# Moving 32x32-turned probability blocks from buffer to buffer in 16 transfers instead of through DRAM

## The reference, cut to what matters

```python
scores = jnp.einsum('bqhd,bkhd->bhqk', q[..., :DN], k) * scale
scores = jnp.where(causal[None, None], scores, NEG_INF)
probs = jax.nn.softmax(scores, axis=-1)
attn = jnp.einsum('bhqk,bkhd->bqhd', probs, v).reshape(B, S, H * DV)
return jnp.einsum('bse,ed->bsd', attn, wo)
```

## Time and profile before

| | us |
|---|---|
| median of 3 runs | 1063.7 (1060.49 to 1066.61) |
| the profiled execution's own time | 1062.6 |
| its span, from the first to the last instruction | 1060.7 |
| TensorE busy | 1047.7 |
| VectorE, GpSimd, ScalarE busy | 808.9, 754.8, 543.0 |

### The profile page before, as it was taken

One profiled execution on the slowest core, in us unless ns is written; L12 is line 12 of the kernel. 1 busy time (PEld: TensorE's weight loads), 2 busy tenths in 40 slices (PEclk: granted clock), 3 DMA queues, 4 the chain that ended last, 5 costly groups with the idle time before them and its releaser, 6 DMA issues. The chain is left out here.

```text
span 1060.7 us, 19733 instructions
## 1 busy us (share of the span) xinstructions
PE 1047.7 (99%) x6025; PEld 918.1 (87%) x6025; DVE 808.9 (76%) x1959; ACT 543.0 (51%) x1573; POOL 754.8 (71%) x1030
## 2 busy tenths in 40 slices
PE   9999999999999999999999999999999999999998
PEld 8888878898898898878988898889888888888987
DVE  7598974467688687877888787878788778778775
ACT  4454321033764555556555555555556555555663
POOL 4777568897957875977597668848774876587920
PEclk9999999999999999999999999999999999999999
DMA  5111242110232333334333423342434333333412
GB/s 168 51 49 52 97 143 70 60 46 21 76 99 82 115 115 99 98 102 132 80 97 118 133 82 96 104 135 75 126 86 123 87 113 111 105 92 109 119 55 79
DMA packets 108120, 100.67 MB, mean 95 GB/s; under 512 B 72688, under 2 KB 88240, under 8 KB 107888
## 3 DMA queue, kind: packets, MB, share of 16 engines
q1 hardware_dynamic: 107728, 98.89, 31.5%
q10 hardware_dynamic: 288, 0.52, 0.1%
HBM read 74.26 MB, written 25.10 MB: 94 GB/s over the span
## 5 line engine op out<-in xcount | busy, mean ns | idle before, releaser
L2063 ACT ACTIVATE prob<-prob,top 128x128 f32<-128x128 f32 (+1 forms) x256 | 114.2, 448 | 85.2 <-DVE top L2096 84.6
L1724 POOL TENSOR_TENSOR form_lo<-wqk_stage,form_hi 128x256 fp32r<-128x256 f32 x192 | 143.5, 748 | 16.0
L2069 ACT ACTIVATE prob<-prob,inv 128x128 f32<-128x128 f32 (+1 forms) x256 | 102.8, 450 | 51.1 <-DVE inv L2102 51.1
L1778 POOL TENSOR_SCALAR vf_hi<-wvo_stage 128x512 fp32r<-128x512 f32 (+1 forms) x48 | 26.6, 554 | 117.4 <-PE banks L200 85.2
L198 PE MATMUL banks<-tT_hi,form_hi 128*128 128x512 f32 x256 | 103.7, 405 | 0.8 <-DVE qT_lo L1851 0.5
L199 PE MATMUL banks<-tT_lo,form_hi 128*128 128x512 f32 x256 | 100.0, 391 | 0.0
L200 PE MATMUL banks<-tT_hi,form_lo 128*128 128x512 f32 x256 | 100.0, 391 | 0.0
L2096 DVE CUSTOM_DVE_ANT_0 prob<-banks,mask 128x128 f32<-128x128 f32 (+1 forms) x256 | 81.0, 353 | 23.0 <-issue 7.6
L2114 DVE TENSOR_TENSOR acc<-acc,banks 128x512 f32<-128x512 f32 x129 | 86.4, 675 | 15.5 <-PE banks L200 14.3
L198 PE MATMUL banks<-wo_hi,oT_hi 128*128 128x512 f32 x240 | 97.1, 404 | 0.7 <-DVE oT_lo L2133 0.7
L199 PE MATMUL banks<-wo_lo,oT_hi 128*128 128x512 f32 x240 | 93.8, 391 | 0.0
(11 more groups left out here) (358 smaller groups left out, 3638.9 us busy)
## 6 DMA issues: line engine op xcount, KB each, us to landing
bounce<-probT SPq DMA_DIRECT2D x117, 192.0 KB, 1.9
pT<-bounce SPq DMA_DIRECT2D x468, 48.0 KB, 1.9
wqk_stage<-in_w_qk SPq DMA_DIRECT2D x32, 512.0 KB, 4.0
wvo_stage<-in_w_v SPq DMA_DIRECT2D x34, 256.0 KB, 3.2
wvo_stage<-in_w_o SPq DMA_DIRECT2D x32, 256.0 KB, 2.9
wd_stage<-in_w_down SPq DMA_DIRECT2D x22, 256.0 KB, 2.6
gu_stage<-in_w_gu SPq DMA_DIRECT2D x10, 512.0 KB, 3.5
out<-acc SPq DMA_DIRECT2D x7, 256.0 KB, 2.0
```

What stands on the lines that cost most here:

```text
L1724: nc.gpsimd.tensor_tensor(form_lo[:, part], src[:, :], as_f32(form_hi[:, part]), ALU.subtract).then_inc(form_ready, 1)
L2063: ins = nc.scalar.activation(pr, pr, ACT.Exp, bias=top[:, n % 2, r:r + 1], scale=-1.0, accum_out=total[:, n % 2, r:r + 1])
L2069: ins = nc.scalar.activation(pr, pr, ACT.Copy, scale=inv[:, n % 2, r:r + 1])
```

## The change

The scratch in DRAM goes. After a turn SyncE waits for `o_done` as before and then issues 16 transfers of 32 partitions x 96 numbers (12 KB), one for each of the four block rows and four block columns, straight from `probT` to `pT`. VectorE's next turn, which waited for the store, waits for all 16 transfers of the pair turned before.

```diff
-        return 64 * len(same_side(g, n))
+        return LANDED * len(same_side(g, n))
...
-        def bounce_pair(g, steps, n):
-
-            turn = bounces(g, n)
-            sp.wait_ge(block_turned, turn + 1)
-            if landings(g, n) > 64:
-                sp.wait_ge(bounce_in[n % 2], landings(g, n) - 64)
-            sp.dma_start(bounce[n % 2], probT[:, :]).then_inc(bounce_out, 16)
-            sp.wait_ge(bounce_out, 16 * (turn + 1))
+        def turn_pair(g, steps, n):
+
+            sp.wait_ge(block_turned, bounces(g, n) + 1)
+            if landings(g, n) > LANDED:
+                sp.wait_ge(pT_landed[n % 2], landings(g, n) - LANDED)
             if g * PAIRS + n >= 2:
                 sp.wait_ge(o_done, g * PAIRS + n - 1)
-            side = P // BLOCKS
+            side, wide = P // BLOCKS, 3 * (P // BLOCKS)
             for c in range(BLOCKS):
-                sp.dma_start(
-                    pT[c * side:(c + 1) * side, n % 2].rearrange("j (a n) -> j a n", a=BLOCKS),
-                    bounce[n % 2][:, c * 3 * side:(c + 1) * 3 * side].rearrange("(a j) n -> j a n", a=BLOCKS),
-                ).then_inc(bounce_in[n % 2], 16)
+                for a in range(BLOCKS):
+                    sp.dma_start(pT[c * side:(c + 1) * side, n % 2, a * wide:(a + 1) * wide],
+                                 probT[a * side:(a + 1) * side, c * wide:(c + 1) * wide],
+                                 ).then_inc(pT_landed[n % 2], 16)
...
-                    act.wait_ge(bounce_in[n % 2], landings(g, n))
+                    act.wait_ge(pT_landed[n % 2], landings(g, n))
...
                     if bounces(g, n):
-                        dve.wait_ge(bounce_out, 16 * bounces(g, n))
+                        last = by_vector[bounces(g, n) - 1]
+                        dve.wait_ge(pT_landed[last % 2], landings(last // PAIRS, last % PAIRS))
```

More of the change, by code:

```diff
@@ L1416, in attention @@
     acc, xT_hi, xT_lo, ident, _, banks, y_done = shared
-    w_qk, w_v, w_o, mask_dram, bounce, out = ins
+    w_qk, w_v, w_o, mask_dram, out = ins
     v_hi, v_lo, v_full, oT_hi, oT_lo, wo_hi, wo_lo, v_rest = late_sb
@@ L1459, in attention @@
     block_turned = sem("block_turned")
-    bounce_out = sem("bounce_out")
-    bounce_in = [sem(f"bounce_in{i}") for i in range(2)]
+    pT_landed = [sem(f"pT_landed{i}") for i in range(2)]
+    LANDED = 16 * BLOCKS * BLOCKS
     pT_hi_done = sem("pT_hi_done")
@@ L1666, in group @@
                 elif kind == "Z":
-                    bounce_pair(g, steps, n)
+                    turn_pair(g, steps, n)
         sp.wait_ge(credit_given, 1)
@@ L2223, in build @@
           w_comb, b_base, b_thr, w_expb, w_qk, w_v, w_o, identity, mask, out):
-    bounce = nc.dram_tensor("bounce", (2, P, 3 * P), F32, kind="Internal").ap()
     with ExitStack() as ctx:
@@ L2305, in build @@
         (sync_1, gpsimd_1, scalar_1, vector_1, tensor_1, gpsimd_ahead, scalar_ahead, vector_ahead, tensor_ahead,
-         credits) = attention(nc, sem, shared, (w_qk, w_v, w_o, mask, bounce, out), (*late_sb, v_rest), lasting_sb, pair_sb,
+         credits) = attention(nc, sem, shared, (w_qk, w_v, w_o, mask, out), (*late_sb, v_rest), lasting_sb, pair_sb,
                               mixed_ready, free)
```

## The result

| | before | after |
|---|---|---|
| median | 1063.2 us (4 runs) | 1828.2 us (1823.5 to 1828.4, 4 runs) |
| profiled execution, its span | 1062.6, 1060.7 | 1828.1, 1825.6 |
| second to last turn | 719.4 us | 1473.8 us |
| per pair turned | 6.26 us | 12.82 us |

The ratio is 1.719 (95% interval 1.7145 to 1.7235): 765 us slower, above the range of 1395 to 1650. Nearly all of it arose between the second turn and the last (304.0 to 1777.8 us), 754 us; 8 us came ahead of it and 2.5 behind.

A forecast was written before the change was run, and what follows sets the result against it. TensorE, 99% busy, was taken to bound the kernel before; after the change, a loop of turn, 16 issues and landing. 367 + 50 + 42 + 4 = +463 us on 1062.6 gave 1526 us, range 1395 to 1650.

The forecast's parts named there:

- the loop: Between second and last turn: 115 turn-to-turn intervals of 9.45 us, 1086.8 us against 719.4, +367 us.
- slow issues: SyncE's occasional slow transfer issues: excess growing with the number of issues, 1872 of them, +50 us, between nothing and this.
- waits for output products: SyncE's `o_done` wait behind the turn: 5.2 us at Z11, 1.8 at Z4, six middle groups, 42 us; bounds nothing to 145.
- first pair, and tail: First pair's landing comes 8.9 us after the turn in place of 5.1, +4 us; the 45 us tail stays.
- I take 0.47: Price in us of one SyncE issue with its gap, taken from the loads that the new transfers replace.
- the upper bound, 0.64: Highest price in us of one issue with its gap, from a small prologue load that took 0.59.
- the far ends of this price: Issue price of 0.35 or 0.64 us in place of 0.47, moving the time by -193 or +274 us.
- The closed loop: Per pair, without overlap: turn 0.57, to first issue 0.02, first to sixteenth issue 6.96, landing 1.9; 9.45 us.
- Landing: Sixteenth transfer's start to its landing: 1.9 us taken; lower end 1.6, 35 us less, nearer which the skill put SBUF copies.
- Rival A: SyncE issues under 0.25 us, TensorE sets the pace, 1055 us; chance 0.05 gain or no change, 0.03 smaller loss.
- Rival B: TensorE's clock falls with idle time: dear form 1769 us, chance 0.07; cheap form costs almost nothing, likelier.
- Rival C: Next turn need not wait for the landing; SyncE's issues alone set 7.4 us per pair, 1194 or 1244 us; chance 0.03.

The follow-up runs named there:

- the test sets: Kernel before, plus sets of four test transfers issued by SyncE behind its last pair; 32 x 96 issues took 0.59 us inside SBUF, 0.42 from DRAM.
- four issues and an open loop: Changed kernel with 4 transfers of 32 x 384 reading a tensor nothing writes, without the turn's wait; 1057.1 us, ratio 0.9959.

## Why the prediction was wrong

The direction and the mechanism were right, and the size of one term was off. The terms in us, measured by the starts of turns and issues in the 115 intervals:

| term | forecast | measured |
|---|---|---|
| the loop: 115 x (9.45 or 11.91) less 719.4 | 367 | 650 |
| slow issues | 50 | 29 |
| waits for output products | 42 | 61 |
| turns that were late for another reason | 0 | 15 |
| first pair, and tail | 4 | 10.5 |
| sum | 463 | 765 |

The failed step is "I take 0.47, because ... size does not set it, and the forms nearest to the new one are the loads that it replaces". In the loop, first issue to sixteenth was 9.41 us and not 6.96: 2.45 x 115 = 282 of the 302 us that were missed. Size indeed does not set it, and neither does the form of these transfers. The ends of the copy do, and the only transfers in the trace of before went between SBUF and DRAM. The step named the upper bound, 0.64, and it was hit almost exactly, but by luck: the row that gave the bound was a load from DRAM to 64 rows, whose price goes with its rows, and no measurement of the new transfer. And the range left the far ends of this price out, though nothing in the trace excluded them. An unseen kind of transfer should have kept both prices inside the range.

- *The closed loop*: right, with TensorE at 64% of the stretch (941.2 of 1482) where two thirds were said. Its other parts were 0.58, 0.03 and 1.89 us against 0.57, 0.02 and 1.9. With the measured price the forecast's own sum gives 1526 + 282 = 1808 us.
- *Landing*: right, and no sooner inside SBUF: a median of 1.8 us for the 16 copies, 1.7 for the same pieces as loads from DRAM. In the test sets a store of 128 x 96 to DRAM landed in a median of 1.6 us, copies of that size inside SBUF in 1.9. The Trainium skill ("DMA: Bandwidth & Descriptors", "Anatomy of one DMA") has the receipt from the target memory as most of the fixed cost, with DRAM the slowest; that section is on transfers that GpSimd issues, and in these, which SyncE issues, the order is not seen.
- *Waits for output products*: the right places, Z4 and Z11 of each middle group, and one more, Z9 of the first. Z4 cost 2.2 us for 1.8, Z11 6.8 to 8.3 for 5.2. Of the 19 us over the forecast Z9 has 2.5; the rest is less than the low clock can have cost by the estimate above. Elsewhere TensorE had run ahead, as said.
- *Late turns*: not foreseen, though the list shows them. The turn behind Z6 came 1.9 us after its transfers had landed in every middle group, because H6, which needs that landing, and P2.5 stand ahead of Z7 on VectorE. The forecast let the next turn wait for the landing alone.
- *Slow issues*: they went with the number of issues less than in proportion: 29 us of excess in 115 sets.
- *Rival A* fell on the price: 0.63 us each against 1.8 to land. The Trainium skill ("DMA: Bandwidth & Descriptors", "Issuing engines are not separate DMA queues") calls the time to initiate a transfer usually small relative to the transfer; 16 of these came to 10 us. The rival's bound on the gain, 7.2 us, stands up: 4.6 was measured with four issues and an open loop.
- *Rival B* came in its cheap form: the granted clock fell to 0.79 in the mean, but without turning TensorE into the bound; by the estimate above it cost some 23 us at most, and a few more in late turns. The Trainium skill ("TensorE: Matmul & The Clock Gate", "Part 1: The HAM clock gate") has the half clock come with idle time, and the trace agrees: it was full throughout before, and below full on the mean where every loop leaves TensorE idle.
- *Rival C*: the wait was in the loop. With it taken out the pace was 10.9 us per pair, not 7.4, again by the price of the issue and not by the sequence.

## What to carry to other kernels

Count transfers by what their issues cost the issuing engine before counting bytes, and price them by transfers between the same two memories; if the trace has none, measure some or keep a wide range. A scratch in DRAM between two buffers is also a second buffer: ask what it decouples before taking it out, here the turn from the output product of two pairs earlier. And when a wait is moved so that a single buffer is held until its last reader has landed, add up the whole loop, with every step that the list puts between the landing and the next use; everything in it then counts in full.

## What was not expected of the hardware

- In a row of like transfers an issue by SyncE, the first aside, took 0.42 to 0.43 us with one end in SBUF and one in DRAM (16, 32, 96 and 128 rows, 4 to 48 KB), 0.59 to 0.62 with both in SBUF (16 to 128 rows, 6 to 64 KB) and 0.60 with both in DRAM (one form, 128 x 96).
- With 64 rows it took 0.60 in each direction between SBUF and DRAM too. No cause was shown for either.
- Part of the price shows in the issue behind: a load of weights straight behind a pair's copies took 0.58 us, all 46 times, and a load straight behind that one 0.43. Straight behind the loads of the kernel before the first takes 0.43 already. Two of the changed kernel's rows stand below.
- Copies inside SBUF of 32 to 128 rows landed in medians of 1.8 to 1.9 us; loads of the same sizes from DRAM in 1.7 to 2.1. There is no clear order.

```profile
513.02 0.58 SPq L1631 DMA_DIRECT2D wqk_stage<-in_w_qk  x1
513.65 0.43 SPq L1635 DMA_DIRECT2D wvo_stage<-in_w_v  x1
```
